# Moving one fold, the cast of the convolution matrix and a pair of row scales in the first block of a one-core kernel

## What is computed

```python
xn = layernorm(x)
K  = s4_kernel(Lambda, p, q, B, Ct, step, 512)        # 512 taps
s  = causal_convolution(xn, K) + D * xn
h1, h3 = lora(xn, w1, A1, B1), lora(xn, w3, A3, B3)   # 512 -> 1376
y  = lora(silu(h1) * h3, w2, A2, B2)                  # 1376 -> 512
out = x + s * silu(y)
# lora(x, w, A, B) = x @ w.T + 2 * (x @ A.T) @ B.T, rank 16
```

## Time and profile before

| | |
|---|---|
| median of 3 executions | 419.93 us (419.90 to 419.93) |
| profiled execution | 420.03 us |
| its span | 418.2 us |
| PE busy | 409.6 us, 98% |
| DVE, ACT, POOL busy | 161.3, 102.5, 65.9 us |
| granted TensorE clock, mean | 0.999 |

### The profile page before, as it was taken

How to read it: one execution, slowest core, us unless ns; L and a number is a source line. 1 busy time by engine, 2 the same in 40 slices (tenths; PEclk the granted TensorE clock), 3 DMA queues, 4 the chain that set the end, 5 groups by cost and what they waited for, 6 DMA issues and landing times.

```text
span 418.2 us, 5041 instructions
## 1 busy us (share of the span) xinstructions
PE 409.6 (98%) x1870; PEld 340.2 (81%) x1870; DVE 161.3 (39%) x251; ACT 102.5 (25%) x168; POOL 65.9 (16%) x132
## 2 busy tenths in 40 slices
PE   8999999999999999999999999999999999999995
PEld 7877888887888888888888888888888888888883
DVE  6856786655493221232234222133225111111115
ACT  7553333322241111122122111112212111111111
POOL 6135626324400104000000101400000000000000
PEclk9999999999999999999999999999999999999999
DMA  8845732330416101000005201000002000000002
GB/s 290 200 155 171 262 98 71 78 99 19 151 52 201 52 0 51 2 0 0 2 25 192 86 0 51 0 0 0 0 0 100 0 0 0 0 0 0 0 0 100
DMA packets 14063, 26.19 MB, mean 63 GB/s; under 512 B 2480, under 2 KB 4208, under 8 KB 14032
## 3 DMA queue, kind: packets, MB, share of 16 engines
q1 hardware_dynamic: 13600, 24.89, 19.0%
q0 software_dynamic: 160, 0.59, 0.4%
q10 hardware_dynamic: 288, 0.52, 0.3%
HBM read 20.37 MB, written 4.53 MB: 60 GB/s over the span
## 4 chain that ended last, share of the span: by engine, by line
PE 93%; DVE 3%; issue 1%; DMA 1%; ACT 1%; DVEq 0%; ACTq 0%
PE h L834 20%; PE h L835 20%; PE h L836 20%; PE f L834 9%; PE f L835 9%; PE f L836 9%; PE spare L821 1%; DVE w L668 1%; DMA lora_first<-lora_dram 1%; DVE raw L658 1%; PE spare L816 1%; DVE gate L723 1%; PE spare L834 0%; PE spare L835 0%; PE spare L836 0%
## 5 line engine op out<-in xcount | busy, mean ns | idle before, releaser
L834 PE MATMUL h<-xt,w 128*128 (+2 forms) x356 | 138.0, 388 | 0.2 <-DVE w L668 0.2
L835 PE MATMUL h<-xt,w 128*128 (+2 forms) x356 | 137.3, 386 | 0.0
L836 PE MATMUL h<-xt,w 128*128 (+2 forms) x356 | 137.3, 386 | 0.0
L710 DVE TENSOR_TENSOR g<-g,h 128x512 f32<-128x512 f32 x44 | 30.3, 688 | 127.2 <-PE h L836 127.2
L834 PEld LDWEIGHTS h<-xt,w 128*128 128x128 f32 x356 | 66.9, 188 | 14.5 <-DVE xt L690 0.8
L836 PEld LDWEIGHTS h<-xt,w 128*128 128x128 f32 x356 | 66.9, 188 | 13.6
L835 PEld LDWEIGHTS h<-xt,w 128*128 128x128 f32 x356 | 66.9, 188 | 13.0
L715 DVE TENSOR_TENSOR ghl<-g,ghl 128x512 fp32r<-128x512 f32 x44 | 31.9, 726 | 99.2 <-ACT ghl L559 99.0
L834 PE MATMUL f<-ghl,w2f 128*128 128x512 f32 x176 | 68.6, 390 | 0.0
L835 PE MATMUL f<-ghl,w2f 128*128 128x512 f32 x176 | 68.5, 389 | 0.0
L559 ACT CAST ghl<-g 128x512 fp32r<-128x512 f32 x44 | 27.3, 621 | 168.0 <-PE f L836 157.4
(11 more groups left out here) (111 smaller groups left out, 269.0 us busy)
## 6 DMA issues: line engine op xcount, KB each, us to landing
raw<-w_dram SPq DMA_DIRECT2D x28, 256.0 KB, 3.8
xres<-xT_dram SPq DMA_DIRECT2D x4, 1024.0 KB, 6.8
outT_dram<-xres SPq DMA_DIRECT2D x16, 256.0 KB, 2.4
rows_next<-x_dram SPq DMA_DIRECT2D x4, 512.0 KB, 3.7
scale_rows<-scales_scratch SPq DMA_DIRECT2D x3, 512.0 KB, 4.1
rows<-x_dram SPq DMA_DIRECT2D x2, 512.0 KB, 6.7
raw<-w_dram SPq DMA_DIRECT2D x4, 224.0 KB, 2.5
lora_stack<-lora_spread_split SPq DMA_DIRECT2D x3, 204.0 KB, 4.0
```

What stands on the lines that cost most here:

```text
L710: nc.vector.tensor_tensor(g[:, :], g[:, :], h3[:, :], ALU.mult).then_inc(g_done, 1)
L834: pe.matmul(out, w[1], m[0], start=start, stop=False)
L835: pe.matmul(out, w[0], m[1], start=False, stop=False)
L836: return pe.matmul(out, w[0], m[0], start=False, stop=stop)
```

## The change

Three edits, all in work of the first block. The up fold (3, 3) leaves the place "down" of tile 1 and stands at "up" of tile 2, ahead of (3, 4). ACT's cast of the convolution matrix moves from "up" of tile 8 to "up" of tile 9. In POOL's queue the second pair of row scales moves ahead of the wait for that cast, and the subtraction is followed by a wait for its own end.

```diff
     if j == 1:
-        return {"gate": [(1, 2)], "up": [(3, 2), (1, 3)], "down": [(2, 1), (3, 3)]}[place]
+        return {"gate": [(1, 2)], "up": [(3, 2), (1, 3)], "down": [(2, 1)]}[place]
+    if j == 2:
+        return {"gate": [(1, 4)], "up": [(3, 3), (3, 4)], "down": [(2, 2)]}[place]
@@
-TOEPLITZ_AT = (8, "up")
+TOEPLITZ_AT = (9, "up")
@@
             pool.wait_ge(xn_ready, RT)
             rows_rstd(1, 0)
+            rows_rstd(1, 2)
             pool.wait_ge(tz_hi, 1)
             tt(tzs[:, 1, :], tz[:, :], tzs[:, 0, :].bitcast(F32), ALU.subtract).then_inc(tz_lo, 1)
-            rows_rstd(1, 2)
+            pool.wait_ge(tz_lo, 1)
             t0, units = group(HT - 1)
```

## The result

The changed kernel takes 424.69 us (median of 4, 424.27 to 425.58) against 419.93 us before (median of 4, measured beside it): a ratio of 1.0115, 95% interval 1.0098 to 1.0133. It is slower, by 4.76 us. The profiled execution took 424.96 us, with a span of 423.2 us.

What follows compares the result with a forecast made beforehand. The prediction took PE's queue as the bound, busy 409.6 of 418.2 us. Its terms, -1.07 - 0.47 + 4.25 = +2.71 us, took the profiled 420.03 us to a forecast of 422.7 us, range 422.2 to 425.0.

Steps and rivals of the forecast that it cites:

- The likeliest case: Whole kernel: the early gains and the new wait before gate(10) add up to 422.7 us; chance 0.63.
- rival (a): Before gate(10): the granted clock falls in PE's wait, costing 2.2 us (0.2 to 4.4), giving 424.9 us; chance 0.20.
- a clock below 1.00 behind the gap: After PE's wait before gate(10): a sign named beforehand that would show the prediction wrong.
- The fold move, -1.07: Tiles 1 and 2 on PE: waits for spare banks vanish, down(1) starts at 36.13 us, 1.07 us earlier.
- POOL's low parts of (3, 3) and (3, 4): Before up(3): POOL's two subtractions end at 41.2 to 41.9 us, due at 42.07, so they stay hidden.
- Rival (b): At up(3) or fold (3, 4): a wait takes back the first gain, giving 423.0 to 423.8 us; chance 0.10.
- The loads behind (3, 5): SP's queue: loads come some 3.2 us later, (1, 6) still lands before its add; cost 0.
- The slack in front of gate(5): Between the add of (1, 6) and gate(5): even a landing 1 us later would only use up slack.
- The freed port, -0.47: Before up(9): without POOL's subtraction beside it, DVE's low part of (3, 10) ends sooner; PE gains 0.39 + 0.08 us.
- The gap, +4.17 and 0.08: Before gate(10): POOL's fills behind the late cast delay PE 4.17 us, plus 0.08 for the first matmul; 4.25 in all.
- The sum of all this, +2.71: Whole kernel: -1.07 - 0.47 + 4.25 = +2.71 us, the change in time without a clock loss.

Runs made afterwards that it cites:

- two kernels without the gap: Fold (3, 3) moved alone, against the kernel before: 419.07 us; the changed kernel with the cast of the matrix back at tile 8: 418.90 us.
- the kernel with 18 matmuls in the gap: The changed kernel with 18 added matmuls on PE, result thrown away, between the folds of tile 9 and the wait for POOL's fills: 422.71 us.
- the kernel with 9 matmuls: The changed kernel with 9 added matmuls on PE between the folds of tile 9 and the wait for POOL's fills: median 422.86 us, in two groups.
- fold (3, 3) back: The changed kernel with fold (3, 3) left at tile 1, so only the two later edits: 426.15 us.
- 5 matmuls: The changed kernel with 5 added matmuls on PE between the folds of tile 9 and the wait for POOL's fills: 424.19 us.
- longer gap: The changed kernel with one more POOL operation, result unused, between the subtraction and the fills: 425.68 us.

## Why the prediction was right, and where it was not

The direction and the range held. The likeliest case, 422.7 us, did not come about; rival (a), 424.9 us, did, and the measured 424.69 us lies at it. It lies within the range only because the upper end had been raised to 425.0 to take in the middle of (a), and one of the prediction's own signs of being wrong, a clock below 1.00 behind the gap, came true. Step by step:

- **The fold move, -1.07.** Down(1) came at 36.09 for 36.13 foretold. Against its own fold (2, 1), which was 0.10 us early, the gain is 1.01. In two kernels without the gap it measures 0.93 and 1.12. Fold (3, 4) waited for nothing.
- **POOL's low parts of (3, 3) and (3, 4).** Foretold for 41.2 to 41.9, due at 42.07. They ended at 41.71, the two together 3.16 us, and up(3) did not wait. The estimate from the row of 1.62 us in the earlier trace rows was the nearer one. Rival (b) was kept off by 0.3 us. The second of the two started 0.07 us behind DVE's `hidden_lo(2)` and took 1.78 us, DVE's operation its usual 0.69.
- **The loads behind (3, 5).** Issued at 39.88 for about 40. For (1, 6) I had it landing in time, 52.6 against 52.98. That step was wrong by a little: it was issued at 42.37 as worked out but took 10.9 us instead of 10.1, and DVE waited for it. The slack in front of gate(5) took that up, as the prediction said it would.

```profile
38.55 3.16 POOL L1007 TENSOR_TENSOR w<-raw,w 128x512 fp32r<-128x512 f32 x2 [4.33 <-ACT w L535]
...
raw<-w_dram SPq DMA_DIRECT2D x1, 256.0 KB, 10.9
...
53.31 0.69 DVE L660 SCALAR_TENSOR_TENSOR raw<-spare,raw 128x512 f32<-128x512 f32 x1 [0.28 <-DMA raw<-w_dram]
...
39.86 0.69 DVE L717 TENSOR_TENSOR ghl<-g,ghl 128x512 fp32r<-128x512 f32 x1 [1.21 <-ACT ghl L561]
...
39.93 1.78 POOL L1007 TENSOR_TENSOR w<-raw,w 128x512 fp32r<-128x512 f32 x1
```

These are POOL's two low parts, the transfer of (1, 6) and DVE's add of it, in the changed kernel, then `hidden_lo(2)` and the second of the two low parts by itself.

- **The freed port, -0.47.** DVE's low part of (3, 10) took 0.62 us instead of 1.73, and PE gained 0.40 + 0.09. The row of the changed kernel:

```profile
96.56 0.62 DVE L670 TENSOR_TENSOR w<-raw,w 128x448 fp32r<-128x448 f32 x1
```

- **The gap, +4.17 and 0.08.** Measured 4.16 in the ledger; the fills ended at 107.93, for 108.04 by the prediction's chain less the 1.54 us gained earlier. Each term had its like one tile earlier, and each held to 0.1 us. The sum of all this, +2.71, is what the kernel with 18 matmuls in the gap measures by the medians: 422.71 - 420.00.
- **The step that failed** is the weighing of rival (a). I read the 4.4 us between the last matmul and the fall of the clock in the earlier trace rows as what an idle time must last, and gave the shorter gap 0.20. That row is one passing of an event whose delay varies: the fall came 4.4 us after the last work there and 2.2 us in the changed kernel. The runs show it lost, by their times and mean clocks, in all sixteen executions with 2.7 us of waiting or more, and in two of six with 1.8. The price I named in (a), 2.2 us, came out close to the 2.32 by the profiles and the 1.98 by the medians, but by luck, out of two errors that cancel: at the lower level the matmuls start 0.43 us apart, not 0.46, and the level lasted 5.0 us of work, not 4.4. Nor is it true that no row shows the way back. In the trace of the kernel before, the first matmuls (128 columns, from 0.99 us on) start 0.213 us apart up to 4.4 us and 0.112 apart from 4.5 us on, a factor of 1.9 and close to the 1.88 between 0.427 and 0.2275. So the clock came up there 3.4 us after PE's first matmul, though the clock column prints 1.00 for all of it. Twelve of these matmuls and then four, in the kernel before (start of the first, time from there to the end of the last):

```profile
1.58 2.77 PE L850 MATMUL h<-g 128*128 128x128 f32 x12
...
4.62 0.61 PE L850 MATMUL h<-g 128*128 128x128 f32 x4
```

- **The Trainium skill** ("TensorE: Matmul & The Clock Gate", section "What's actually happening") had been cited for a slow default and a rhythm that doesn't start with the kernel. The runs fit both: PE's first matmuls go at the slower pace in the trace of the kernel before (0.213 us apart, then 0.112), and the kernel with 9 matmuls kept the clock in four executions and lost it in two. The Trainium skill's port rule ("SBUF — State Buffer", section "SBUF: two separate sides") says that the later one waits for the whole instruction. The traces agree but for 0.14 us. In the 1.73 us row DVE came 0.04 us behind POOL, which still had 1.25 us to run, and took 1.11 longer than its 0.62. POOL's second low part of the two came when DVE had 0.62 us left, and took 0.48 longer than its 1.30. The row of 1.62 us in the earlier trace rows, which the prediction took for a partial delay, is the same case: DVE, at its low part of a fold, had 0.47 us left, and POOL took 0.33 longer than 1.29.

What stays open is what makes the delay of the clock's fall vary.

## What to carry to other kernels

Before an operation is moved later, read the queue behind it on every engine that waits for it, and find who waits for the last entry: here the subtraction was done at 98.93 us and first used at 113.72, but the three fills behind it had only 3 us to spare. In a kernel whose TensorE is never idle, price a new wait twice, by its length and by the clock it may cost; stops of 2.7 to 5.1 us here made the stage behind them 1.6 to 2.4 us longer in the profiles (gate(10) took 4.44 to 5.26 us for 2.83 at full clock). Where a queue must wait, put the work that doesn't depend on it ahead of the wait, which here turned a loss of 4.8 us into a gain of 1.5.

## What the runs showed of the hardware

- The time from TensorE's last matmul to the fall of the granted clock is not fixed. In the four profiles in which it fell in or at the end of the gap it was 2.2 us (changed kernel), 2.5 (fold (3, 3) back), 2.7 (5 matmuls) and 3.0 (longer gap). Behind the last work of a kernel it was 4.4 us before and 2.2 in the changed kernel, and with 9 matmuls the clock was still at 2.4 GHz 5.0 us after. By the times and mean clocks it was lost in two of six executions with 1.8 us of waiting, in four of four with 2.7, and in all twelve with 4.0 or 5.1.
- At the lower level matmuls of 512 columns start 0.427 us apart, against 0.2275 at the full one: a factor of 1.88, not 2. The slow stretch of work lasted 5.0 and 5.3 us behind gaps of 4.0 us, 4.7 behind one of 5.1 and 3.4 behind one of 2.7.
- Of two operations by DVE and POOL that each read two SBUF tensors, the later one lost the time that the earlier one still had to run, less 0.14 us, in three cases (1.11 of 1.25 us, 0.48 of 0.62, 0.33 of 0.47).
- A fill by POOL (a write only) did not delay DVE's operations on two SBUF tensors: the one of w2f beside DVE's two low parts in the changed kernel took 0.95 us, as it did in the earlier trace rows, and DVE's two took 0.69 and 0.68 us, where one without a fill beside it took 0.69 (at 98.47 us). The row shows the two merged:

```profile
106.69 1.29 DVE L670 TENSOR_TENSOR w2f<-raw,w2f 128x512 fp32r<-128x512 f32 x2 [0.15 <-DVE raw L660]
```
